# A mixture-of-experts kernel: rows loaded to places by expert, outputs in six buffers

## The chip, the cores and the metric

The kernel runs on one core of a Trainium2 chip. The time is that of one execution on the device, in microseconds (us); the kernel before took 328.78 us, the median of three runs (328.36 to 329.91). A core has five engines, each with its own queue of instructions: TensorE (PE in the profile; PEld is its weight load), VectorE (DVE), ScalarE (ACT), GpSimd (POOL) and SyncE (SP), which here only issues DMAs. Sixteen DMA engines move data between memory (HBM) and the core's SBUF. Engines wait for each other through semaphores.

## The reference

```
x = x + xattn(layernorm(x), ctx)             # x is (8, 100, 512), ctx is (8, 722, 512)
    # x1 = h @ ctx.T ; t = gelu_tanh(x1) * x1 ; result t @ ctx
x = x + ffn(layernorm(x))
    # logits = h @ router_w (512 x 16); assign = argmax(logits); w = sigmoid(top logit)
    # hh = gelu(h @ w1[assign] + b1[assign])          w1 is (16, 512, 1024)
    # out = (hh @ w2[assign] + b2[assign]) * w        w2 is (16, 1024, 512)
```

All numbers are float32. Each of the 800 tokens goes to one of 16 experts, which is known only when the kernel runs.

## The kernel before

First come eight batches of attention. For each, TensorE makes the products with the context (L316, L323), VectorE adds the residual and takes mean and variance, and the router's logits give each token its expert and its rank in the expert. GpSimd then scatters the 100 rows of the batch (values, gate, mean, inverse deviation, output row number) into `rows`, a tensor in memory with a region of 832 rows for each expert (L804). Four scatters of blank rows pad the regions (L843).

Then comes the expert stage. Work is cut into units of 32 rows of one expert. Units 0 to 3 (the head) are the first 32 rows of experts 0 to 3, read from `rows` before the last batches are done. All other units follow in the order of the experts, as many for each as it has rows. A unit j needs: its rows in SBUF; `next_tokens` (VectorE, L672), a normalization into `cur`; a transpose on TensorE (L404) and a copy to `curT` (L677); `first_layer` (L385, 32 matmuls with W1); `hidden_units` (VectorE transpose, L682), `hidden_bias` (L688), a Gelu on ScalarE (L491); `second_layer` (L396, 64 matmuls with W2); `residual_bias` (L694), which adds the gated b2 to the rows; `finish` (VectorE, L705), which writes the result to `y_out`; and a scatter to the output by GpSimd (L860). TensorE's order is first layer of j, transpose of j+1, second layer of j-1. The second layer of a unit waits until the `finish` of the unit before it has read the bank `p_y`.

Weights lie in four slots, expert e in slot e modulo 4; W1 and W2 of an expert are 2 MB each, loaded by SyncE as two halves (L232). All halves of experts 0 to 3 are loaded during the attention, as `EARLY` spreads them over the batches. In the loop at L285, W1 of an expert waits until the last unit of the slot's expert before it has passed its first layer (L291), W2 until it has passed its second (L294).

In the kernel before, each unit has its own place in `xr`, and its column in `rows` is a number that must be read from a table (`colof`). SyncE loads unit 4 (L274), GpSimd all others (L213): three for units 5 to 7, then two in each round, mixed with the output scatters. There are two output buffers. In `scatter_unit`, GpSimd waits until the scatter of two units ago has landed, frees its buffer for VectorE (`s_y_free`, L855), copies the row numbers into `out_at` (L856), waits for `finish`, and issues the scatter. In each round it then waits for the loads that it issued in this round (`s_ld`, L893) and reports two more units as landed (`s_land`, L894), for which VectorE's `next_tokens` waits (L666).

## Time and profile before

| | |
|---|---|
| median of three runs | 328.78 us |
| the profiled execution | 326.27 us |
| its span (first to last instruction) | 324.6 us |
| TensorE busy | 253.4 us (78%) |
| VectorE busy | 113.0 us (35%) |
| GpSimd busy | 89.0 us (27%) |
| ScalarE busy | 32.4 us (10%) |
| moved by DMA | 100.93 MB, mean 311 GB/s |
| weight DMAs (L232) | 64 of 1 MB |
| loads of rows of units 4 and on | 27 by GpSimd, 1 by SyncE, 66 KB each |
| output scatters (L860) | 32 |

The 64 weight DMAs are 67 MB, 48 of them for experts 4 to 15. The 32 scatters are the 32 units. The page cuts the span in 40 slices of 8.1 us, and slice 0 is the first. A row of the timeline gives the start, the time taken, the engine, the line and the tiles, and in square brackets how long the engine was idle before it and what ended that.

### The profile page before, as it was taken

What the parts mean: (1) busy time and instruction counts of PE and PEld (TensorE: products, weight loads), DVE (VectorE), ACT (ScalarE), POOL (GpSimd) and SP (SyncE); (2) the same over time, 40 slices, a digit from 0 to 9 for tenths busy, and PEclk for the clock granted to TensorE, in tenths of its full rate; (3) what the DMA queues carried; (4) which work ended last, traced back from release to release, by engine and by line L of the source; (5) the groups of instructions that cost most, each with busy time, mean ns of one, the idle gap of its engine ahead of it and who ended that gap; (6) DMA issues with size and microseconds to landing.
All of it is one profiled execution on the core that took longest, in us unless ns stands there. A gap on an engine that the chain in (4) does not pass through costs nothing. (4 is left out here: it accounts for less than half of the span.)

```text
span 324.6 us, 9969 instructions
## 1 busy us (share of the span) xinstructions
PE 253.4 (78%) x3763; PEld 179.8 (55%) x3764; DVE 113.0 (35%) x385; ACT 32.4 (10%) x76; POOL 89.0 (27%) x141
## 2 busy tenths in 40 slices
PE   1899999999999898784663747840197999899982
PEld 0868867867867456553431544520175766566762
DVE  2134444444442663242210222220043344344430
ACT  0311111112011021010000000000010111011110
POOL 1002312312341353533330234413022122221222
PEclk9999999999999959995979569895579999999998
DMA  7999899999999998753999806599759999999700
GB/s 252 377 357 361 287 371 343 385 378 342 418 381 309 420 418 327 121 182 138 291 403 361 305 25 236 176 364 375 245 209 424 424 423 426 420 421 424 289 16 14
DMA packets 21437, 100.93 MB, mean 311 GB/s; under 512 B 4942, under 2 KB 6882, under 8 KB 12200
## 3 DMA queue, kind: packets, MB, share of 16 engines
q1 hardware_dynamic: 16680, 93.81, 77.0%
q0 software_dynamic: 4592, 6.56, 6.6%
q8 instruction: 14, 0.23, 0.3%
q10 hardware_dynamic: 144, 0.27, 0.2%
q14 instruction: 7, 0.06, 0.1%
HBM read 95.89 MB, written 5.14 MB: 311 GB/s over the span
## 5 line engine op out<-in xcount | busy, mean ns | idle before, releaser
L396 PE MATMUL bank<-W,area 128*32 128x128 f32 x2048 | 76.2, 295 | 41.3 <-DVE area L705 38.5
L396 PEld LDWEIGHTS bank<-W,area 128*32 128x32 f32 x2048 | 61.9, 118 | 51.5 <-DVE area L705 40.3
L385 PE MATMUL bank<-W,area 128*32 128x256 f32 x1024 | 69.0, 409 | 14.9 <-issue 14.5
L385 PEld LDWEIGHTS bank<-W,area 128*32 128x32 f32 x1024 | 37.1, 117 | 36.8 <-issue 24.6
L860 POOL DMA_INDIRECT out<-area,out_at x32 | 32.4, 1012 | 72.1 <-DVE area L705 57.8
L316 PEld LDWEIGHTS bank<-xnT,area 128*128 128x128 f32 (+1 forms) x384 | 44.7, 194 | 4.7 <-issue 4.7
L323 PE MATMUL bank<-area,hidT 128*100 128x512 f32 (+1 forms) x96 | 46.8, 601 | 0.0
L316 PE MATMUL bank<-xnT,area 128*128 128x100 f32 (+1 forms) x384 | 45.1, 280 | 1.4 <-issue 1.4
L705 DVE SCALAR_TENSOR_TENSOR area<-bank,area 128x128 f32 (+1 forms) x28 | 9.8, 351 | 86.7 <-POOLq L855 65.8
L213 POOL DMA_DIRECT2D area<-rows x27 | 19.2, 711 | 53.5 <-issue 53.5
L491 ACT ACTIVATE area<-area 128x256 f32<-128x256 f32 x32 | 13.4, 417 | 187.6 <-PE bank L396 177.5
L682 DVE STREAM_TRANSPOSE area<-bank 128x256 f32<-128x256 f32 x32 | 14.4, 449 | 39.6 <-PE bank L385 28.4
L804 POOL DMA_INDIRECT rows<-row,pos x8 | 8.7, 1082 | 49.6 <-DVE pos L569 32.6
L323 PEld LDWEIGHTS bank<-area,hidT 128*100 128x100 f32 (+1 forms) x96 | 13.7, 167 | 10.0 <-issue 10.0
L525 DVE TENSOR_TENSOR hidT<-hidT,bank 128x300 f32<-128x300 f32 x16 | 7.4, 464 | 19.5 <-ACT hidT L463 19.5
L688 DVE TENSOR_TENSOR area<-area,b1s 128x256 f32<-128x256 f32 x32 | 13.6, 424 | 0.2 <-DVE area L682 0.2
L404 PEld LDWEIGHTS bank<-con,area 128*128 128x128 f32 x33 | 4.7, 142 | 14.7 <-issue 14.6
L672 DVE TENSOR_SCALAR area<-area 128x128 f32 (+1 forms) x28 | 9.8, 350 | 7.7 <-DMA area<-rows 3.9
L463 ACT ACTIVATE hidT<-bank 128x300 f32<-128x300 f32 x16 | 6.8, 422 | 56.4 <-PE bank L316 56.4
L792 POOL TENSOR_TENSOR rs_x<-ve_x,con 100x1 f32<-100x1 f32 x8 | 4.5, 558 | 25.9 <-DVE ve_x L511 25.9
L404 PE MATMUL bank<-con,area 128*128 128x128 f32 x33 | 11.2, 341 | 0.1
L792 POOL TENSOR_TENSOR row<-ve_t,con 100x4 f32<-100x4 f32 x8 | 8.4, 1049 | 9.2 <-DVE ve_t L511 9.0
(95 smaller groups left out, 146.0 us busy)
## 6 DMA issues: line engine op xcount, KB each, us to landing
W<-in_w SPq DMA_DIRECT2D x64, 1024.0 KB, 11.9
area<-in_ctx_main SPq DMA_DIRECT2D x8, 1280.0 KB
area<-in_ctxT_a SPq DMA_DIRECT2D x8, 768.0 KB, 8.8
area<-in_ctxT_b SPq DMA_DIRECT2D x8, 676.0 KB, 8.0
area<-rows POOLq DMA_DIRECT2D x27, 66.0 KB, 7.1
xs<-in_x SPq DMA_DIRECT2D x8, 200.0 KB
area<-in_ctx_rest SPq DMA_DIRECT2D x8, 160.0 KB
xs<-in_b SPq DMA_DIRECT2D x4, 192.0 KB
```

Source lines behind the costliest of these rows:

```text
L213: eng.dma_start(xr[:, at, :].rearrange("p o d -> p (o d)"), rows[bass.ds(col * U, U), :].rearrange("t (q d) -> q t d", q=Q)).then_inc(sign ...
L316: last = nc.tensor.matmul((p_xa, p_xb)[part][0:n, T * c:T * c + T], ctxTs[b % 2][part][:, k, P * c:P * c + n], xnT[:, k, :], start=(k == 0 ...
L323: last = nc.tensor.matmul(p_att[0:T, :], hidT[0:CW[c], c, :], cxs[b % 2][0:CW[c], c, :], start=(c == 0), stop=(c == SC - 1))
L385: last = nc.tensor.matmul(p_h[U * q:U * q + U, 0:FQ], curT[:, U * k:U * k + U], mine, start=(k == 0), stop=(k == KD - 1), tile_position=(0 ...
L396: last = nc.tensor.matmul(p_y[U * q:U * q + U, 0:DQ], hT[:, U * c:U * c + U], W2[:, slot, c, DQ * q:DQ * q + DQ], start=(c == 0), stop=(c ...
L404: nc.tensor.transpose(p_blk[:, 0:P], cur, ident).then_inc(s_blk, 1)
L491: nc.scalar.activation(hT, h_pre, ACT.Gelu).then_inc(s_act, 1)
L672: nc.vector.tensor_scalar(cur, mine[:, 0:DQ], mine[:, DQ + 1:DQ + 2], mine[:, DQ + 2:DQ + 3], ALU.subtract, ALU.mult).then_inc(s_next, 1)
L682: nc.vector.transpose(h_pre, p_h[:, 0:FQ]).then_inc(s_hT, 1)
L688: nc.vector.tensor_tensor(view, view, bias.unsqueeze(3).to_broadcast([P, 2, Q, U]), ALU.add).then_inc(s_hb, 1)
L792: nc.gpsimd.tensor_tensor(rs, ve, neg_half.to_broadcast(list(rs.shape)), ALU.pow).then_inc(s_rs, 1)
L860: nc.gpsimd.indirect_dma_start(out_q, bass.IndirectOffsetOnAxis(ap=out_at[r][:, :], axis=0), y_out[:, r, :], None, bounds_check=last_out, ...
```

## The change

- **Places.** `xr` now has a place for each expert (0 to 15), which holds the first unit of that expert that isn't a head unit, one that isn't used, and 24 places for further units (the extras). The first kind starts at a fixed row of the expert's region, so SyncE loads them without a table: `load_first`, four DMAs (one for each quarter of a row) for experts 0 to 3, four for 4 to 7, four for 8 to 15. Each waits for the pad scatters of its experts.
- **Extras.** GpSimd loads these (`load_extra`): two before scatter 1, four (`AHEAD` is 6) before scatter 2, and the rest (at least one) between scatters 3 and 4.
- **A table.** `packed` has one number for each unit, with its expert and the places of itself, of the unit before it and of the one two behind. VectorE reads it once for a unit and takes the fields out by shifts and masks. It is made by more steps in `units_of` and by a small matmul with the constant `packing` on TensorE in place of two transposes.
- **Outputs.** `y_out` and `out_at` have six buffers: one for each head unit, used once, and two for all others in turn. VectorE now copies the row numbers, in `finish`.
- **Waits.** VectorE waits for the loads at fixed points: `s_first[0]` before the tokens of unit 4, `s_extra[0]` before those of unit 5, `s_extra[1]` before unit 4, the four further extras and `s_first[1]` before unit 5, the b2 of experts 4 to 15 before unit 6, `s_first[2]` and all other extras before unit 9.
- **SyncE and GpSimd queues.** The constants (in two parts), the router, b1 (in two parts) and b2 of the head are loaded by GpSimd at the start and not by SyncE. `EARLY` has two halves less in its last entry; these two follow behind the first `load_first`.
- `b2_copy` stands behind `hidden_bias` of unit 1.

```diff
-EARLY = (0, 0, 1, 1, 1, 2, 4, 7)
+EARLY = (0, 0, 1, 1, 1, 2, 4, 5)
...
-        def load_unit(eng, j, signal):
-            at = bass.ds(j, 1) if not isinstance(j, int) else slice(j, j + 1)
+        def load_extra(eng, k, signal):
+            at, place = (slice(i, i + 1) if isinstance(k, int) else bass.ds(i, 1) for i in (k, k + E + 1))
             col = eng.value_load(colof[0:1, at], min_val=0, max_val=E * PER - 1)
-            eng.dma_start(xr[:, at, :].rearrange("p o d -> p (o d)"),
+            eng.dma_start(xr[:, place, :].rearrange("p o d -> p (o d)"),
                           rows[bass.ds(col * U, U), :].rearrange("t (q d) -> q t d", q=Q)).then_inc(signal, 16)
 
...
+            def load_first(lo, hi, skip, signal):
+                for q in range(Q):
+                    sp.dma_start(xr[U * q:U * q + U, lo:hi, :],
+                                 rows.rearrange("(e n) d -> n e d", e=E)[skip:skip + U, lo:hi, XW * q:XW * q + XW]
+                                 ).then_inc(signal, 16)
+
             sp.wait_ge(s_att, NB)
             for i in range(RB):
                 sp.wait_ge(s_row[i], 16 * len(range(i, NB, RB)))
             sp.wait_ge(s_pad[0], 16)
-            sp.dma_start(xr[:, SLOTS, :], rows[U:2 * U, :].rearrange("t (q d) -> q t d", q=Q)).then_inc(s_own[0], 16)
+            load_first(0, SLOTS, U, s_first[0])
+            load_weights(4 * SLOTS - sum(EARLY))
+            sp.wait_ge(s_pad[1], 16)
+            load_first(SLOTS, 2 * SLOTS, 0, s_first[1])
 
             sp.wait_ge(s_x2, NB)
             sp.wait_ge(s_xnps, NB)
...
+            for i in range(2, PADS):
+                sp.wait_ge(s_pad[i], 16)
+            load_first(2 * SLOTS, E, 0, s_first[2])
...
+                number = dve.value_load(packed[0:1, at], min_val=0, max_val=(1 << 22) - 1)
+
+                def field(bit):
+                    part = number // (1 << bit)
+                    return place_of(nc.s_assert_within(dve.snap(part % 64 if bit < 16 else part), 0, PLACES - 1,
+                                                       skip_runtime_bounds_check_because="places end there"))
+                return bass.ds(dve.snap(number % E), 1), field(10), field(4), field(16)
+
...
-            def finish(j, r):
+            def finish(j, mine):
+                r = dve.snap(j % 2 + SLOTS) if not isinstance(j, int) else j if j < SLOTS else j % 2 + SLOTS
                 at = slice(r, r + 1) if isinstance(r, int) else bass.ds(r, 1)
-                mine = place_of(j)
+                dve.wait_ge(s_y_free, j + 1)
                 dve.wait_ge(s_prep, j + 1)
-                dve.wait_ge(s_y_free, j + 1)
+                apart()
+                nc.vector.tensor_copy(out_at[:, at], mine[:, DQ + 3:DQ + 4].bitcast(U32)).then_inc(s_out_at, 1)
                 dve.wait_ge(s_y, j + 2)
                 apart()
...
+            dve.wait_ge(s_extra[1], 16)
+            unit(SLOTS, e4, head_of(3), place_of(0), after4)
+            dve.wait_ge(s_ahead, 16 * (AHEAD - 2))
+            dve.wait_ge(s_first[1], 16 * Q)
+            unit(SLOTS + 1, e5, before5, mine5, after5)
+            dve.wait_ge(s_b2_rest, 16 * Q)
+            with dve.Fori(SLOTS + 2, SLOTS + AHEAD - 1) as j:
+                unit(j, *unit_of(j))
+            more_loads = dve.value_load(counts[0:1, 1:2], min_val=1, max_val=EXTRA - AHEAD)
+            dve.wait_ge(s_first[2], 16 * Q)
+            dve.wait_ge(s_more, 16 * more_loads)
+            apart()
+
+            others = dve.value_load(counts[0:1, 0:1], min_val=E, max_val=E + EXTRA)
...
+            for lo, hi in ((C_ONE, C_PAD), (C_PAD, C_ALL)):
+                pool.dma_start(con[:, lo:hi], consts[:, lo:hi]).then_inc(s_conl, 16)
+            pool.dma_start(rw[:, :, :], router).then_inc(s_rw, 16)
+            for lo in range(0, E, E // 2):
+                pool.dma_start(b1s[:, lo:lo + E // 2, :], b1[:, lo:lo + E // 2, :]).then_inc(s_b1, 16)
+            pool.dma_start(b2q[:, :, :], b2[0:SLOTS].rearrange("e (q d) -> q e d", q=Q)).then_inc(s_b2, 16)
+            pool.wait_ge(s_conl, 32)
...
-            def scatter_unit(j, r, before):
-                at = slice(j, j + 1) if isinstance(j, int) else bass.ds(j, 1)
-                mine = head if isinstance(j, int) and j < SLOTS else xr
-                pool.wait_ge(s_next, j + 1)
-                if before is not None:
-                    pool.wait_ge(s_done[r], before)
-                apart()
-                if before is not None:
-                    pool.sem_inc(s_y_free, 1)
-                nc.gpsimd.tensor_copy(out_at[r][:, :], mine[:, at, DQ + 3].bitcast(U32)).then_inc(s_out_at, 1)
+            def scatter_unit(j, r, done):
                 pool.wait_ge(s_out_at, j + 1)
                 pool.wait_ge(s_yo, j + 3)
                 apart()
...
-                nc.gpsimd.indirect_dma_start(out_q, bass.IndirectOffsetOnAxis(ap=out_at[r][:, :], axis=0),
+                nc.gpsimd.indirect_dma_start(out_q, bass.IndirectOffsetOnAxis(ap=out_at[:, r:r + 1], axis=0),
                                              y_out[:, r, :], None, bounds_check=last_out, oob_is_err=False
-                                             ).then_inc(s_done[r], 16)
-
-            scatter_unit(0, 0, None)
-            pool.wait_ge(s_blank, 1)
+                                             ).then_inc(done, 16)
+
+            scatter_unit(0, 0, s_head_done)
             for i in range(RB):
                 pool.wait_ge(s_row[i], 16 * len(range(i, NB, RB)))
                 apart()
...
+            for i in range(PADS):
                 pool.wait_ge(s_pad[i], 16)
                 apart()
-
-            for j in range(2, SLOTS):
-                for k in range(2):
-                    load_unit(pool, OWN + 2 * (j - 2) + k, s_ld)
-                scatter_unit(j, j % 2, 16 * (j // 2))
-                pool.wait_ge(s_ld, 32 * (j - 1))
-                pool.sem_inc(s_land, 2)
-            n = units(pool)
-            less = pool.value_load(n_less[0:1, 0:1], min_val=SLOTS + E - NEAR - 1, max_val=MAXU - NEAR - 1)
-            loading, pairs = pool.snap(less // 4), pool.snap((less + (NEAR - 2)) // 2)
-            with pool.Fori(0, loading) as i:
+            pool.wait_ge(s_eof, 2)
+            for k in range(2):
+                load_extra(pool, k, s_extra[k])
+            scatter_unit(1, 1, s_head_done)
...
+            more_loads = pool.value_load(counts[0:1, 1:2], min_val=1, max_val=EXTRA - AHEAD)
+            with pool.Fori(AHEAD, more_loads + AHEAD) as k:
+                load_extra(pool, k, s_more)
+            pairs = pool.snap((pool.value_load(counts[0:1, 0:1], min_val=E, max_val=E + EXTRA) + 1) // 2)
+            for r in range(2):
...
+            with pool.Fori(1, pairs) as i:
                 for r in range(2):
-                    for k in range(2):
-                        load_unit(pool, 4 * i + (NEAR + 2 * r + k), s_ld)
-                    scatter_unit(2 * i + (SLOTS + r), r, 16 * i + 32)
-                    pool.wait_ge(s_ld, 64 * i + (16 * (NEAR - OWN) + 32 * r + 32))
-                    pool.sem_inc(s_land, 2)
-            with pool.Fori(4 * loading + NEAR, n) as j:
-                load_unit(pool, j, s_ld)
```

How the change moves instructions, at three places. On GpSimd, the steady loop over units before (one half of it, for one unit; L213 loads rows, L850 frees, L860 scatters):

```order
L213 DMA area<-rows 128x1x132
L850 ISA
L852 ISA
L856 ISA
L856 COPY out_at<-area 128x1
L858 REGISTER_ALU
L860 DMA out<-area,out_at 3200x128
L893 ISA
L212 ISA
L212 TENSOR_LOAD colof
```

and now, with both halves (L913 and L914 are the waits, L916 scatters):

```order
L941 ISA
L913 ISA
L914 REGISTER_ALU
L916 DMA out<-area,out_at 3200x128
L913 REGISTER_ALU
L914 REGISTER_ALU
L916 DMA out<-area,out_at 3200x128
L941 ISA
L941 COMPARE_AND_BRANCH
```

The loads, the table reads and the copy have gone from the loop. On SyncE, from the last early weights to the first weights of expert 4 before (W is the weight slots, in_b is b2):

```order
L232 DMA W<-in_w 128x2048 x11
L274 DMA area<-rows 128x1x132
L279 DMA xs<-in_b 32x12x128 x4
L285 UNCONDITIONAL_BRANCH
L285 ISA
L287 TENSOR_LOAD ends
```

and now:

```order
L249 DMA W<-in_w 128x2048 x9
L284 DMA area<-rows 32x4x132 x4
L249 DMA W<-in_w 128x2048 x2
L284 DMA area<-rows 32x4x132 x4
L300 DMA xs<-in_b 32x12x128 x4
L284 DMA area<-rows 32x8x132 x4
L309 UNCONDITIONAL_BRANCH
L309 ISA
L311 TENSOR_LOAD ends
```

Twelve row loads and two weight halves stand where one row load stood. On VectorE, the end of a unit in the steady loop before (L694 is `residual_bias`, L705 `finish`):

```order
L694 SCALAR_TENSOR_TENSOR area<-xs,area 128x128
L705 ISA x2
L705 REGISTER_ALU
L705 SCALAR_TENSOR_TENSOR area<-bank,area 128x128
L765 ISA
L765 COMPARE_AND_BRANCH
```

and now:

```order
L735 SCALAR_TENSOR_TENSOR area<-xs,area 128x128
L745 ISA x2
L745 COPY out_at<-area 128x1
L748 ISA x2
L748 SCALAR_TENSOR_TENSOR area<-bank,area 128x128
L826 ISA
L826 COMPARE_AND_BRANCH
```

The copy of the row numbers (L745) has come to VectorE.

## Rows read from the trace of the kernel before

**Rows 1.** The page, section 2: what the DMA engines moved, in 40 slices

```profile
GB/s 252 377 357 361 287 371 343 385 378 342 418 381 309 420 418 327 121 182 138 291 403 361 305 25 236 176 364 375 245 209 424 424 423 426 420 421 424 289 16 14
```

**Rows 2.** Busy time by stretch: stretch, length, engines, then PEclk, DMA share, GB/s

```profile
140.60:237.70 97.10, 52.06 (x942) 35.57 (x945) 19.89 (x60) 3.76 (x9) 27.19 (x42) 0.76 0.74 259
237.70:306.00 68.30, 62.42 (x1439) 44.33 (x1437) 29.58 (x88) 6.27 (x15) 17.44 (x29) 0.99 0.99 410
```

**Rows 3.** The waits: who, for whom, us in total, times, the longest

```profile
DVE area L705 <- POOLq L855: 65.8, 9, 20.7
...
PE bank L396 <- DVE area L705: 38.5, 10, 19.0
...
SPq L232 <- PE bank L396: 81.5, 12, 22.3
```

**Rows 4.** Timeline of GpSimd and VectorE, 177 to 189 us

```profile
177.30 0.75 POOL L213 DMA_DIRECT2D area<-rows  x1 [7.02 <-issue]
178.68 0.68 POOL L213 DMA_DIRECT2D area<-rows  x1 [0.63 <-issue]
...
179.47 0.35 DVE L705 SCALAR_TENSOR_TENSOR area<-bank,area 128x128 f32 x1 [8.33 <-POOLq L855]
...
188.24 0.74 POOL L213 DMA_DIRECT2D area<-rows  x1 [6.48 <-issue]
```

**Rows 5.** First layers from 237 us on, counted, and rows of the timeline

```profile
L385 PE MATMUL bank<-W,area x544: 376/379/634, 237.6 to 313.1; 128*32 128x256 f32 x182
...
237.65 2.89 PE L385 MATMUL bank<-W,area 128*32 128x256 f32 x32
...
298.30 1.93 PE L385 MATMUL bank<-W,area 128*32 128x256 f32 x32 [0.51 <-issue]
...
311.57 1.93 PE L385 MATMUL bank<-W,area 128*32 128x256 f32 x32 [0.47 <-issue]
...
319.19 0.35 DVE L705 SCALAR_TENSOR_TENSOR area<-bank,area 128x128 f32 x1 [2.74 <-PE bank L396]
```

**Rows 6.** Timeline at the first weight load of the loop, and its landing

```profile
140.61 0.38 SPq L232 DMA_DIRECT2D W<-in_w  x1
...
141.23 0.45 DVE L682 STREAM_TRANSPOSE area<-bank 128x256 f32<-128x256 f32 x1 [0.39 <-issue]
...
143.23 2.02 PE L385 MATMUL bank<-W,area 128*32 128x256 f32 x32 [0.38 <-issue]
...
DMA to landing us min/median/max: 9.3/9.3/9.3
```

**Rows 7.** Busy time by stretch, 126 to 140.6 us, and VectorE's timeline

```profile
126.00:134.00 8.00, 6.42 (x177) 5.10 (x181) 3.04 (x12) 0.83 (x2) 4.38 (x7) 1.00 0.92 198
134.00:140.60 6.60, 5.80 (x122) 3.38 (x110) 2.52 (x9) 0.42 (x1) 3.12 (x6) 1.00 0.26 52
...
137.78 0.45 DVE L682 STREAM_TRANSPOSE area<-bank 128x256 f32<-128x256 f32 x1 [2.47 <-issue]
```

**Rows 8.** Timeline of the full-rate stretch: `finish`, transpose, scatter and its return

```profile
262.30 0.35 DVE L705 SCALAR_TENSOR_TENSOR area<-bank,area 128x128 f32 x1 [0.88 <-PE bank L396]
...
263.49 0.98 POOL L860 DMA_INDIRECT out<-area,out_at  x1 [2.42 <-DVE area L705]
...
270.04 0.18 POOL L856 COPY out_at<-area 128x1 uint32 x1 [1.24 <-DMA out<-area,out_at]
...
276.93 0.45 DVE L682 STREAM_TRANSPOSE area<-bank 128x256 f32<-128x256 f32 x1 [0.96 <-PE bank L385]
```

**Rows 9.** Timeline: the last of four row loads, and what waited for them

```profile
224.40 0.68 POOL L213 DMA_DIRECT2D area<-rows  x1 [1.10 <-issue]
...
233.28 0.18 POOL L856 COPY out_at<-area 128x1 uint32 x1 [8.20 <-DMA area<-rows]
```

**Rows 10.** SyncE's weight loads from 237 us on, and the stretch of the stream's end

```profile
237.77 47.83 SPq L232 DMA_DIRECT2D W<-in_w  x26
...
306.00:308.00 2.00, 2.00 (x52) 1.40 (x46) 0.96 (x3) 0.42 (x1) 0.18 (x1) 1.00 0.10 33
```

More of the change, by code:

```diff
@@ L422, in _ @@
             first_layer(2, 2, 16)
-            pe.wait_ge(s_tab, 10)
+            pe.wait_ge(s_tab, 16)
             pe.wait_ge(s_pos, NB)
-            for i in range(2):
-                last = nc.tensor.transpose(p_rk[0:1, 64 * i:64 * i + MAXU], unit_f[:, i:i + 1], ident[0:MAXU, 0:MAXU])
-            last.then_inc(s_eofps, 1)
+            nc.tensor.matmul(p_rk[0:1, 0:MAXU], unit_f[:, 0:1], ident[0:MAXU, 0:MAXU], start=True, stop=False)
+            nc.tensor.matmul(p_rk[0:1, 0:MAXU], unit_f[:, 1:2], packing, start=False, stop=True)
+            nc.tensor.matmul(p_rk[0:1, 64:64 + EXTRA], unit_f[:, 2:3], picked[:, :], start=True, stop=True
+                             ).then_inc(s_eofps, 1)
             transpose_tokens(3)
@@ L723, in _ @@
             pads()
-            b2_copy()
             units_of()
@@ L758, in unit @@
                 hidden_bias(j, e)
-                next_tokens(j + 2)
-                residual_bias(j, e)
-                finish(j - 1, (j + 1) % 2 if isinstance(j, int) else dve.snap((j + 1) % 2))
-            for j in range(SLOTS, OWN - 2):
-                unit(j)
-            with dve.Fori(OWN - 2, last) as j:
-                unit(j)
-            e = expert_of(last)
+                next_tokens(j + 2, following)
+                residual_bias(e, mine)
+                finish(j - 1, before)
+            dve.wait_ge(s_extra[1], 16)
[11 more added lines that the diff above has]
+            others = dve.value_load(counts[0:1, 0:1], min_val=E, max_val=E + EXTRA)
+            last = others + (SLOTS - 2)
+            with dve.Fori(SLOTS + AHEAD - 1, last) as j:
+                unit(j, *unit_of(j))
+            e, before, mine, _ = unit_of(last)
             hidden_units(last)
@@ L895, in _ @@
-            with pool.Fori(4 * loading + NEAR, n) as j:
-                load_unit(pool, j, s_ld)
-            pool.wait_ge(s_ld, 16 * less + 16 * (NEAR + 1 - OWN))
-            pool.sem_inc(s_land, 4)
-            with pool.Fori(loading, pairs) as i:
-                for r in range(2):
-                    scatter_unit(2 * i + (SLOTS + r), r, 16 * i + 32)
+            pool.wait_ge(s_eof, 2)
+            for k in range(2):
+                load_extra(pool, k, s_extra[k])
+            scatter_unit(1, 1, s_head_done)
```

190 lines of the change are left out of this document (105 added, 85 removed).

## The prediction

> **What bounds the kernel now.** I read the slices of the page first, then the waits, the busy times by stretch, and the timeline around the longest waits.
>
> The GB/s row [rows 1] splits the run in three: some 120 us of attention, most slices above 340; a stretch up to slice 29 (243 us) in which it keeps falling, once to 25; and 60 us at 424 GB/s. The middle stretch, 140.6 to 237.7 us, has the TensorE busy for 52 of 97 us and the DMA at 0.74 of its time; the next one has 0.99 and 410 GB/s [rows 2]. So the expert stage is not bound by weights until 237 us; something else holds it there.
>
> The waits name it [rows 3]: VectorE's `finish` (L705) waited 65.8 us for GpSimd's queue at L855, the increment that frees an output buffer; TensorE's second layer waited 38.5 us for that `finish`; and SyncE's weight loads waited 81.5 us for that second layer. The timeline shows one round, which is one unit [rows 4]: GpSimd issues two loads at 177.30 and 178.68 us, and only behind them frees the buffer, so L705 runs at 179.47 after 8.33 us idle; then comes the scatter, and then GpSimd waits until both loads have landed, so the next round starts at 188.24, 10.9 us later. Behind 237.7 us no loads are left and the pace is another one: 544 L385 matmuls are 17 first layers of 32, the first at 237.65 and the last at 311.57 us [rows 5]. That is 73.9 / 16 = 4.62 us for a unit, and there the same two output buffers are in use.
>
> **What the change removes.** GpSimd no longer mixes loads with scatters, no longer copies the row numbers (VectorE does), and the wait for `s_ld` before releasing rows is gone. Of the 28 loads of rows, 16 come by SyncE in 12 DMAs, 12 by GpSimd, six of these before unit 4 and six in one piece before scatter 4. By the routing of these inputs (from the reference) the experts have 2,1,1,4,1,1,1,2,1,3,1,2,2,2,3,1 units behind the four head units; expert 0's last is unit 5, expert 3's unit 11, and expert 14's first unit 28. If the hold-up is gone, late are (a) TensorE at 4.62 us a unit, (b) the weights of experts 4 to 15, 48 DMAs of 1.049 MB, which start when unit 5 has left its first layer (140.61 us before, [rows 6]).
>
> **The front, up to the first weight load.** Two of the sixteen early weight DMAs move behind the attention, about 5 us of DMA (2.1 MB at 424 GB/s), and their consumer, the second layer of unit 3, ran at 135.6 us. The row loads of SyncE are 1.06 MB in pieces of 528 B. The nearest rows are the b2 pieces and row loads between 126 and 134 us: 198 GB/s at a share of 0.92; from 134 to 140.6 us the share was 0.26, 4.9 us of it free [rows 7]. Bounds for 1.06 MB: 2.5 us at 424 GB/s and 5.3 us at 198; less 1.9 us for the loads that it replaces there. I take 5, most of which the free 4.9 us hide. Unit 4's token wait is unlikely to grow, since the last row scatter has 5 us less of weights ahead. VectorE waited 2.47 us before the transpose of unit 4 at 137.78 [rows 7] on the b2 pieces; that wait moves behind unit 5, and two table reads (about 1 us each by the 0.96 us before L682 in the steady loop, [rows 8]) stand in its place. First layer of unit 5: unchanged, ends at 140.4. But before unit 5's transpose (141.23 us, [rows 6]) VectorE now waits for four loads that GpSimd issues behind scatter 1, at about 131.5 to 136.2 us (1.16 us apart). Four loads with weights in flight took until 233.28 us after the last issue at 224.40 [rows 9], 8.9 us; with nothing in flight about 7. So they land at 143 to 145: a wait of 2 to 4 us, I take 3. The first-layer start of unit 6 goes from 143.23 to 146.2, and its second layer for unit 5 ends 4.3 us later at 150.5.
>
> The constants, router and biases go by six GpSimd DMAs at about 7 to 13 us instead of SyncE's queue. Their reader is free until 16.7 us; I cost it at nothing, bounds 1 us gained (0.45 MB less ahead of the second batch) and 2 us lost.
>
> **The unit loop.** The added copy on VectorE is at most 0.25 us and 4 register operations; it stands before the wait for the second layer, which was 0.88 us long [rows 8]. Price 0; if that cover were gone, 26 x 0.25 = 6.5 us. The stretch with six loads in one piece: GpSimd issues them from 143 to 151 us (1.38 us each in its loop, from 177.30 to 178.68 [rows 4]), scatters 4 and 5 at 151 and 152.5 us. Unit 6 needs scatter 4 landed. In the full-rate stretch a scatter issued at 263.49 us released GpSimd at 270.04 [rows 8], 6.5 us; with loads ahead 8.9 at most. So `finish(6)` runs at about 160 us against 153 by pace: one wait of 7 us. Then first layer of unit 9 at 162.4, of unit 31 at 162.4 + 22 x 4.62 = 264. From that start to the end of the span 324.6 - 311.57 = 13.0 us [rows 5]. TensorE's bound: 277 us of span.
>
> **The weight stream.** The W2 of expert 4 may go when the second layer of unit 5 is done, 150.5, issue at 150.8. The two DMAs of a tensor on an idle queue took 9.3 us to land [rows 6], the second issued 0.5 later: W2 of expert 4 is there at 160.6. Afterwards full rate: from 237.77 us 26 DMAs were issued and the stream ended at about 306 us [rows 10], 28.0 MB in all at 410 GB/s including the ramp, 424 without it [rows 1]; outputs take 3 in 100 of that, so 1.049 / 0.412 = 2.54 us for one. Up to the W1 of expert 14 are 19 more tensors, 38 x 2.54 = 96.5; the six loads cost 0.6 us each (the DMA dropped from 424 to about 310 GB/s for 8 us around four of them, slices 27 and 28 [rows 1]), 3.6. It lands at 160.6 + 96.5 + 3.6 = 260.7 us. No slot is late: expert 3's slot is free at about 173.5 us, its turn comes near 180. Unit 28 can begin its first layer some 0.5 us before (the wait is by halves), and from 298.30, unit 28 before, to the end were 26.3 us [rows 5]. Span: 260.7 - 0.5 + 26.3 = 286.5 us.
>
> So the weights, not TensorE (277), set the end. The profiled execution of before took 326.27 us, 1.67 over its span, and the median of the three is 328.78, 2.5 more. 286.5 + 1.7 = 288.2 us profiled, 290.7 beside the median. Since the front has more small gains than I booked (a shorter wait for unit 4's rows, 1.7 us), I say **289 us**; its own range 283 to 296.
>
> The Trainium skill, DMA: Bandwidth & Descriptors, section Specifications, gives an HBM limit of about 358 GB/s for a core. The trace disagrees: 420 to 426 GB/s for 55 us [rows 1]. By the page a DMA of weights would last 2.93 us, the 40 up to expert 14's W1 cost 16 us more, and the time would be 305.
>
> The same page, Anatomy of one DMA, fits a GpSimd DMA as 2.0 us plus its bytes at 436 GB/s, an estimate of 2.2 us for a scatter of 66 KB. The trace shows 6.5 us under load [rows 8]. By the page the output ring could never bind and the 7 us wait at unit 6 would be none, which leaves the sum as it is, since the weights are later.
>
> **The rivals.**
> - *TensorE is the bound.* The front loses nothing (3 us), the loads cost no DMA time (3.6 us), the stream starts by 145 us. Then 277 to 279 of span, **282 us**. For it: much of the first tensor's 9.3 us may be waiting behind the small pieces. Against: expert 14's three units stand right behind their weights.
> - *The front collides.* SyncE's queue reaches the first weight only behind 12 row loads and 4 b2 loads, and the small pieces run at 120 GB/s instead of 198 (128 to 136 us before had 154). 8.8 + 5 us of work against 4.9 free, and the four loads land at 149: unit 5 waits 8 us, the stream starts 8 late. **298 us**.
> - *The output ring binds, on the slower side.* Each pair of units now waits for the scatter of two units ago: 0.35 finish + 1.2 to the issue + landing + 0.4. With 6.5 us that is 8.5, under 2 x 4.62 = 9.24. With more it sets the pace: finish 29 would come at 164 + 12 pairs, and finish 31 and the end (5.4 us behind it, 319.19 to 324.6, [rows 5]) right after. A landing of 9.3 us, as the weights had, gives 11.3 per pair and 309 us of time; 11 us gives 13.0 and 329, the time of before; from there on the kernel is slower, at 12.5 us 14.5 and **347 us**. For it: the 8.9 us at the loads, with weights in flight. Against: between 240 and 306 us the stream had no gap either, and scatters were back in 6.5 us.
> - *The stream runs at 358 GB/s*: **305 us**, against the rate seen here.
>
> **Chances.** Forecast 0.58, TensorE 0.18, collision 0.16, 358 GB/s 0.01, ring 0.07, of which 0.04 slower and 0.02 within 0.5%. The range, 280 to 303, takes the first three. A measurement tells 0.5% (1.6 us). Faster 0.94, within 0.5% 0.02, slower 0.04.
>
> **What would show it.** Right: L705 hardly waits for GpSimd but once, around 155 us, for 5 to 9 us; DMA above 415 GB/s from about 155 to 268 us; first layers 4.6 us apart on the mean; the last 26 us as before; one wait of 2 to 4 us ahead of unit 5's transpose. Wrong: waits of L705 for GpSimd in many units (the ring), DMA holes past 160 us (slots free late), a first weight load after 145 us (the front), or first layers that never wait for a DMA (TensorE).

## The result, and the profile after

The changed kernel takes **296.05 us** (median of 4 runs, 293.97 to 298.72), the kernel before 329.35 (328.36 to 335.05) beside it: a ratio of 0.898, 95% interval 0.890 to 0.906. The forecast was 289 us with a range of 280 to 303. The profiled execution is the longest of the four, 298.72 us with a span of 296.2 (the others 292.3 to 295.3); it counts as a slow run, as does the 335.05 us of the kernel before, and the ratio leaves both out. At the median the time missed the forecast by 7 us. The trace is of the long execution, and its span is 9.7 us over the forecast's span of 286.5 us; the terms below are for these 9.7 us, and up to 3.9 of them are its own excess over its fellows.

The page's GB/s row, 40 slices of 7.4 us, is the one to set against [rows 1]:

```profile
GB/s 232 378 382 361 295 332 391 378 355 366 364 420 387 329 395 412 227 342 168 86 340 330 416 417 281 287 370 422 424 424 420 423 422 423 418 422 424 343 17 7
```

The full rate no longer begins at slice 30 (243 us) but at slice 27 (200 us), and nearly at slice 22 (163 us); between them two slices stand at 281 and 287. Busy time by stretch (columns as in [rows 2]) shows the same with the engines:

```profile
140.60:160.00 19.40, 14.94 (x299) 10.65 (x303) 6.16 (x22) 1.25 (x3) 8.26 (x10) 0.85 0.78 242
160.00:180.00 20.00, 14.91 (x323) 10.28 (x317) 6.73 (x22) 1.25 (x3) 2.05 (x3) 0.90 1.01 401
180.00:200.00 20.00, 17.15 (x407) 12.08 (x403) 10.10 (x32) 1.67 (x4) 4.74 (x5) 1.00 0.80 302
200.00:280.00 80.00, 70.44 (x1597) 48.94 (x1593) 36.82 (x115) 7.08 (x17) 15.52 (x16) 0.96 1.01 422
```

The weight stream (the DMAs of weights, one behind the other) is the bound from 200 us on: 422 GB/s for 80 us. The waits that held the kernel before [rows 3] have these successors (L745 and L748 are the two operations of `finish`, L409 the first layer, L420 the second, L249 the weight load):

```profile
PE bank L409 <- issue: 19.6, 16, 4.3
...
PE bank L409 <- DMA W<-in_w: 3.0, 3, 1.6
...
DVE out_at L745 <- POOLq L945: 5.1, 2, 4.0
...
DVE area L714 <- DMA area<-rows: 4.3, 1, 4.3
```

```profile
SPq L249 <- PE bank L420: 46.3, 11, 8.2
...
SPq L249 <- PE bank L409: 21.7, 4, 10.1
```

`finish` waits 5.1 us for GpSimd instead of 65.8, and TensorE's second layer waits for `finish` only 1.4 us in all, against 38.5. The first layers now wait for weights, three times and 3.0 us in all: 0.87 us in unit 26, 0.57 and 1.57 us in unit 28. So the weights set the end, but with TensorE close behind. SyncE's weight loads still wait for TensorE, 10.1 us at most; the question is whether the DMA engines run dry meanwhile. The front, by the timeline:

```profile
139.36 0.34 DVE L714 TENSOR_SCALAR area<-area 128x128 f32 x1 [4.34 <-DMA area<-rows]
...
143.76 1.90 PE L409 MATMUL bank<-W,area 128*32 128x256 f32 x32
...
145.88 1.30 SPq L249 DMA_DIRECT2D W<-in_w  x2
```

VectorE waited 4.34 us for the first of GpSimd's loads (issued at 129.1), which landed 9.7 us after its issue, so the first layer of unit 5 and the first weight load behind it are some 5 us later than before (145.88 against 140.61, [rows 6]). Then comes the stretch in which TensorE falls behind:

```profile
152.37 12.42 SPq L249 DMA_DIRECT2D W<-in_w  x8
...
156.34 2.92 PE L409 MATMUL bank<-W,area 128*32 128x256 f32 x32 [4.04 <-issue]
156.92 1.04 POOL L916 DMA_INDIRECT out<-area,out_at  x1 [0.92 <-issue]
...
165.85 0.15 DVE L745 COPY out_at<-area  x1 [3.98 <-POOLq L945]
...
168.11 2.36 PE L409 MATMUL bank<-W,area 128*32 128x256 f32 x20 [4.31 <-issue]
...
172.85 1.91 PE L409 MATMUL bank<-W,area 128*32 128x256 f32 x32
```

Unit 7's first layer starts 4.04 us late at 156.34, and unit 8's stops after some of its matmuls and goes on at 168.11, 4.31 us later. Both waits are "issue": no semaphore that the profile shows ended them. `finish(6)` waits 3.98 us for a scatter that was issued at 156.92, behind the six row loads, and came back 8.9 us later. Unit 9 starts at 172.85. Now units 11 and 12 (the last of expert 3, and the one behind it), the weight loads in the same time, and the DMA engines:

```profile
181.81 1.93 PE L409 MATMUL bank<-W,area 128*32 128x256 f32 x32
...
187.56 1.93 PE L409 MATMUL bank<-W,area 128*32 128x256 f32 x32 [1.59 <-issue]
...
189.69 1.95 PE L420 MATMUL bank<-W,area 128*32 128x128 f32 x64
```

```profile
183.95 0.94 SPq L249 DMA_DIRECT2D W<-in_w  x2
...
191.70 0.81 SPq L249 DMA_DIRECT2D W<-in_w  x2
```

```profile
182.00:187.00 5.00, 3.97 (x97) 2.72 (x89) 2.76 (x9) 0.53 (x2) 0.97 (x1) 1.00 0.52 156
187.00:190.00 3.00, 2.44 (x45) 1.43 (x49) 0.37 (x1) 0.00 (x0) 0.97 (x1) 1.00 1.01 426
190.00:195.00 5.00, 4.52 (x122) 3.39 (x117) 2.11 (x8) 0.42 (x1) 0.97 (x1) 1.00 0.66 215
```

The W1 slot of expert 3 is free when unit 11's first layer is through, 183.7, and its next load leaves at 183.95; the W2 slot when unit 11's second layer is through (the 64 L420 from 189.69 on), and its load leaves at 191.70. Each time the queue had drained: the rate of the stretch is 156 and 215 GB/s, and 3.1 and 2.5 us of stream are lost, 5.6 in the two holes together. The end, to set against [rows 5]:

```profile
263.42 1.07 PE L409 MATMUL bank<-W,area 128*32 128x256 f32 x16 [0.57 <-DMA W<-in_w]
...
266.06 1.69 PE L409 MATMUL bank<-W,area 128*32 128x256 f32 x16 [1.57 <-DMA W<-in_w]
...
279.20 1.93 PE L409 MATMUL bank<-W,area 128*32 128x256 f32 x32 [0.45 <-issue]
...
287.06 0.35 DVE L748 SCALAR_TENSOR_TENSOR area<-bank,area 128x128 f32 x1 [1.58 <-PE bank L420]
288.25 0.97 POOL L916 DMA_INDIRECT out<-area,out_at  x1 [2.26 <-DVEq L845]
```

Unit 28 waits for its W1 by halves, as forecast, but it starts at 263.42 us, where the sum had 260.2, and its second half waits until 266.06. From unit 31's start the end is 17.0 us away; before it was 13.0. GpSimd's last instruction, a DRAIN, takes 5.46 us from 290.54 on; before it took 1.70 us.

### The profile page after: what moved, and what is told of

Read it like the earlier page. It is cut to its first block, busy times and chain, and to the rows that moved or that the text cites. A ratio compares the mean times of both kernels' runs of the same rounds, so it can differ in the third digit from the quotient of the medians.

```text
span 296.2 us, 9809 instructions
## 1 busy us (share of the span) xinstructions
PE 245.5 (83%) x3767; PEld 174.1 (59%) x3768; DVE 120.7 (41%) x425; ACT 32.4 (11%) x76; POOL 74.0 (25%) x99
## 4 chain that ended last, share of the span: by engine, by line
PE 70%; DMA 13%; issue 9%; DVE 2%; SPq 2%; POOL 1%; DVEq 0%; POOLq 0%
PE bank L409 17%; PE bank L420 17%; PE bank L340 15%; PE bank L347 14%; DMA W<-in_w 9%; DMA area<-rows 3%; PE bank L428 2%; PE bank L355 1%; SPq L249 1%; PE bank L325 1%; DMA xs<-in_x 1%; PE bank L331 1%; PE bank L363 0%; DVE area L724 0%; PE bank L362 0%
## 5 line engine op out<-in xcount | busy, mean ns | idle before, releaser
L409 PE MATMUL bank<-W,area 128*32 128x256 f32 x1024 | 68.6, 408 | 22.8 <-issue 19.6
L420 PE MATMUL bank<-W,area 128*32 128x128 f32 x2048 | 70.4, 282 | 6.8 <-issue 5.3
L420 PEld LDWEIGHTS bank<-W,area 128*32 128x32 f32 x2048 | 58.2, 113 | 14.9 <-issue 9.6
L409 PEld LDWEIGHTS bank<-W,area 128*32 128x32 f32 x1024 | 36.1, 115 | 44.0 <-issue 27.0
L916 POOL DMA_INDIRECT out<-area,out_at x32 | 31.3, 978 | 117.4 <-DVE area L748 113.6
L748 DVE SCALAR_TENSOR_TENSOR area<-bank,area 128x128 f32 (+1 forms) x28 | 9.8, 351 | 10.2 <-issue 5.5
L230 POOL DMA_DIRECT2D area<-rows x12 | 8.4, 703 | 10.7 <-issue 10.7
L325 PE MATMUL bank<-con,xs 100*128 100x100 f32 x32 | 4.5, 265 | 7.4 <-DVE xs L544 7.4
```

The lines of the kernel that those rows point to most:

```text
L409: last = nc.tensor.matmul(p_h[U * q:U * q + U, 0:FQ], curT[:, U * k:U * k + U], mine, start=(k == 0), stop=(k == KD - 1), tile_position=(0 ...
L420: last = nc.tensor.matmul(p_y[U * q:U * q + U, 0:DQ], hT[:, U * c:U * c + U], W2[:, slot, c, DQ * q:DQ * q + DQ], start=(c == 0), stop=(c ...
L748: nc.vector.scalar_tensor_tensor(out=y_out[:, at, :].rearrange("p o d -> p (o d)"), in0=p_y[:, 0:DQ], scalar=mine[:, DQ:DQ + 1], in1=mine[ ...
L916: nc.gpsimd.indirect_dma_start(out_q, bass.IndirectOffsetOnAxis(ap=out_at[:, r:r + 1], axis=0), y_out[:, r, :], None, bounds_check=last_ou ...
```

## The experiments

Two theories on the stream. **H**: TensorE is some 10 us late at unit 9, so expert 3's slots (the expert with most units) come free late, the DMA engines run dry at 182 and 190 us, and since the stream is the bound behind them, each us lost there is a us at the end. **R**: the end is set by rate and row loads alone, and the holes are made up for. On the last 4 us: **D**, GpSimd's drain is longer because it writes nothing itself in the loop any more. Each kernel below ran in four executions; the kernel before ran beside them, at 328.26 us with kernels 1, 3, 4 and 5, 327.67 with 2, 6, 7 and 8, and 321.81 with 9 to 12. The changed kernel itself ran in none of these rounds. Between groups, then, neither ratios nor differences of 1 or 2% in time say much, and the traces have to carry the comparison.

The table gives, for the profiled execution of the changed kernel and of the experiments made from it: when the weight stream's first load was issued, how many us it lost between 160 and 200 us (40 x (1 - GB/s / 422), from the rate in that window), their sum, the first us in which the DMA was below 150 GB/s at the end, the span, and the drain with the number of GpSimd's DMAs.

| kernel | median us (range) | first load | lost | sum | stream's end | span | drain us (DMAs) |
|---|---|---|---|---|---|---|---|
| changed kernel | 296.05 (293.97–298.72) | 145.9 | 6.7 | 152.6 | 280 | 296.2 | 5.46 (66) |
| two buffers | 296.09 (294.70–296.82) | 143.9 | 6.8 | 150.7 | 279 | 292.6 | 5.46 (66) |
| last six loads by SyncE | 294.45 (294.08–294.65) | 153.9 | 0.1 | 154.0 | 278 | 292.6 | 4.97 (60) |
| late b2 | 295.11 (293.88–297.05) | 144.4 | 6.3 | 150.7 | 281 | 295.3 | 5.46 (66) |
| loads in pairs | 296.78 (295.56–299.96) | 143.1 | 7.0 | 150.1 | 280 | 293.9 | 5.54 (67) |
| early list as before | 296.66 (293.19–298.62) | 140.9 | 7.1 | 148.0 | 277 | 291.5 | 5.46 (66) |
| GpSimd write | 295.38 (295.09–295.88) | 144.1 | 6.5 | 150.6 | 279 | 293.2 | 5.46 (66) |
| delay in unit 9 | 304.06 (303.91–304.95) | 142.9 | 15.3 | 158.2 | 287 | 302.5 | 5.46 (66) |
| delay in unit 14 | 293.45 (292.78–294.86) | 145.6 | 5.3 | 150.9 | 279 | 293.1 | 5.46 (66) |
| constants by SyncE, early list | 292.52 (289.58–295.40) | 141.4 | 4.8 | 146.2 | 275 | 287.9 | 4.96 (60) |
| constants and last six by SyncE | 295.35 (294.91–297.04) | 156.2 | 0.0 | 156.2 | 280 | 293.3 | 4.48 (54) |

**1. The kernel before with the scatter ahead of the loads.** The loads' landing is waited for two rounds later.

```
+ pool.wait_ge(s_ld[r], 32 * i + 32); pool.sem_inc(s_land, 2)   # now ahead of the scatter
  scatter_unit(2 * i + (SLOTS + r), r, 16 * i + 32)
+ for k in range(2): load_unit(pool, 4 * i + (NEAR + 2 * r + k), s_ld[r])   # was ahead of it
```

> The kernel before with one thing altered: in GpSimd's rounds the output scatter goes first and the two loads of rows behind it, and a pair of loads is waited for two rounds later, not in its own round. Places by unit, the load of unit 4 by SyncE alone and two output buffers stay. Theory L (the gain came from taking the loads' landing out of the buffer's way): most of it is here too, 298 to 306 us, since only the loads' issue (1.4 us each) and a scatter landing behind loads (about 9 us a pair of units) are left in nine rounds. Rival P (fixed places, SyncE and six buffers carry it): 315 us or more.

Measured: 314.48 us (310.51 to 315.76), ratio 0.954 (0.945 to 0.963). What is left of the wait sits in one place, as the waits of this kernel say:

```profile
DVE area L705 <- POOLq L855: 31.9, 4, 23.8
```

That is 31.9 us against 65.8 [rows 3], with 23.8 at once, at unit 13, where GpSimd waits for the last four loads before it frees a buffer. So the order of loads and scatters is part of the gain, but not the half of it (13.8 of 33 us). The time is at the bound of rival P's 315 us and far from L's 298 to 306.

**2. The same with that last wait one pair of scatters later.**

```
- pool.wait_ge(s_ld[2], ...); pool.sem_inc(s_land, 4)           # here before
  with pool.Fori(loading, loading + 1) as i: scatter_unit(...) x2
+ pool.wait_ge(s_ld[2], ...); pool.sem_inc(s_land, 4)
```

> The kernel before with scatters ahead of loads as in the first experiment, and the wait for the last four loads moved behind one more pair of scatters. In the first experiment one wait of finish for that moment was 23.8 us of the 31.9 in all. Theory L (taking the landing out of the buffer's way is the gain): 294 to 299 us, the changed kernel's time with none of its places, table and buffers. Rival P: the stream would fill the gap anyway, 308 us or more.

Measured: 307.17 us (305.40 to 313.22), ratio 0.935 (0.926 to 0.944); its waits:

```profile
DVE area L705 <- POOLq L855: 25.9, 5, 16.0
```

L's 294 to 299 us did not come; P's 308 missed by 0.8. 16 us at once remain, again behind the landing of loads in GpSimd's order. Still, about 20 of the 33 us come with this much, with none of the places, the table or the six buffers, so taking the loads out of the way of the output buffers is the larger part of the gain. The other 11 to 13 us were not separated further.

**3. The changed kernel with two output buffers instead of six.**

```
- r = j % 2 + SLOTS        # finish: four buffers of their own for units 0 to 3
+ r = j % 2
- pool.sem_inc(s_y_free, SLOTS + 2)
+ pool.sem_inc(s_y_free, 2)
```

> The changed kernel with two output buffers for all units in place of six. Theory L: the four head buffers hide only landings while little else is late, so 296 to 299 us against 296. Rival B (the buffers carry a good part): GpSimd waits for scatters 0 and 1 before it frees units 2 and 3, each some 8 us, and the first weight load starts late: 304 us or more.

Measured: 296.09 us, ratio 0.901 (0.895 to 0.908). The waits for a buffer grow to

```profile
DVE out_at L745 <- POOLq L953: 8.9, 3, 7.2
```

and the time doesn't, as theory L had it. The six buffers are worth nothing here that these runs can tell (the interval is 0.7% to either side), and the rival of the output ring falls with them.

**4. The last six row loads by SyncE, ahead of the weight loop.**

```
+ sp.wait_ge(s_eof, 2)                 # SyncE, ahead of its weight loop
+ with sp.Fori(AHEAD, more_loads + AHEAD) as k: load_extra(sp, k, s_more)
- with pool.Fori(AHEAD, more_loads + AHEAD) as k: load_extra(pool, k, s_more)
```

> The changed kernel with the six last extras loaded by SyncE ahead of its weight loop and not by GpSimd between scatters 3 and 4. Theory H (TensorE, late by ten microseconds at unit 9, frees expert 3's slot late, and the two holes that this opens in the weight stream at 182 and 190 us move the end one for one): the 4 us wait of finish for a buffer at unit 6 goes, the holes shrink by about 4 us, 290 to 293 us. Rival R (the end is set by the rate of the stream and what the row loads cost it, the holes are filled up anyway): 295 to 297 us.

Measured: 294.45 us, ratio 0.897 (0.891 to 0.903). Timeline of SyncE, and the window 160 to 200 us:

```profile
141.15 11.45 SPq L230 DMA_DIRECT2D area<-rows  x6
153.92 2.16 SPq L249 DMA_DIRECT2D W<-in_w  x4
```

```profile
160.00:200.00 40.00, 33.51 (x797) 24.98 (x798) 17.96 (x56) 3.33 (x8) 7.71 (x8) 1.00 1.01 421
```

The stream starts 8 us later and loses nothing between 160 and 200 us, and the kernel ends no later. So the changed kernel's early start is given back in the holes. Two things close them here: the slots' turn comes later, and TensorE is through unit 11's first layer at 177.22 us instead of 183.7, since its waits in units 7 and 8 are 2.89 and 2.80 us instead of 4.04 and 4.31 (L413 is the first layer here):

```profile
152.67 2.71 PE L413 MATMUL bank<-W,area 128*32 128x256 f32 x32 [2.89 <-issue]
...
162.42 1.50 PE L413 MATMUL bank<-W,area 128*32 128x256 f32 x23 [2.80 <-issue]
```

The time lies between H's 290 to 293 us and R's 295 to 297.

**5. b2 of the later experts by ScalarE, later.** The four b2 loads leave SyncE's queue and are issued by ScalarE behind its unit 4.

```
- sp.dma_start(b2s[U * q:U * q + U, SLOTS:, :], ...)    # SyncE
+ act.dma_start(b2s[U * q:U * q + U, SLOTS:, :], ...)   # ScalarE, behind gelu_unit(4)
```

> The changed kernel with the b2 of experts 4 to 15 (four DMAs in pieces of 512 bytes) issued by ScalarE behind unit 4's Gelu and waited for before unit 9, not by SyncE at 127 us. Theory H: the extra load that unit 5 waits for lands 3 to 4 us earlier, all of units 5 to 11 come as much earlier, the stream starts earlier and the holes stay: 292 to 294 us. Rival R: the b2 pieces now take their DMA time from the weight stream, nothing gained: 296 to 299 us.

Measured: 295.11 us, ratio 0.898 (0.891 to 0.905): VectorE still waits 4.3 us for its row load, and the holes stay (6.3 us). The b2 pieces do not make the front late, so H's 292 to 294 us, which rested on that, did not come, nor did R's 296 to 299.

**6. The six loads in pairs behind scatters 3, 4 and 5** instead of in one piece, so that `finish(6)` gets its buffer sooner.

```
  for r in range(2):
      scatter_unit(SLOTS + r, SLOTS + r, s_done[r])
+     for k in range(AHEAD + 2 + 2 * r, AHEAD + 4 + 2 * r): load_extra(pool, k, s_mid)
```

> The changed kernel with the six last extras in three pairs, behind scatters 3, 4 and 5, and one more load behind them; VectorE waits for the six before unit 9. SyncE's queue stays as in the changed kernel, so the first weight load keeps its place at about 146 us. Theory H: no wait of finish for a buffer at unit 6, units 9 to 11 some 4 us earlier, expert 3's slot free earlier, the holes in the stream at 182 and 190 us about half as long: 291 to 294 us. Rival F (the 4 us are under the stall of unit 8's first layer, in which TensorE waits for no semaphore at all, and come back nowhere): 295 to 297 us.

Measured: 296.78 us, ratio 0.908 (0.900 to 0.916). The longest wait of `finish` for a buffer falls from 4.0 to 1.1 us and unit 9 still starts at 172.6 (172.85 in the changed kernel): that wait lay beside TensorE's own stall in unit 8 and cost nothing. This is rival F's number and reason; H's 291 to 294 us had taken unit 9 to be 4 us earlier.

**7. The early list of weight loads as before** (seven instead of five in its last entry).

```
- EARLY = (0, 0, 1, 1, 1, 2, 4, 5)
+ EARLY = (0, 0, 1, 1, 1, 2, 4, 7)
```

> The changed kernel with EARLY as before: all sixteen early weight DMAs are issued by the end of the attention. Theory Q (the extra load of unit 5 lands 10 us after its issue since 2 MB of weights and the small pieces go at the same time): the rows' scatters land later by up to 3 us, but the load for unit 5 is as late as without, 295 to 298 us. Rival: the two halves are what makes it late, then unit 5 starts 4 us earlier and the time is 291 to 293 us.

Measured: 296.66 us with a wide range (293.19 to 298.62), ratio 0.906 (0.899 to 0.913): no difference that these runs can tell. The median is where theory Q had it; the profiled execution, the fastest of the four at 293.19, is nearer to the rival: the stream starts 5.0 us earlier (140.9) and ends 3 us earlier.

**8. A write by GpSimd ahead of each scatter of the loop.**

```
+ nc.gpsimd.memset(touched[:, :], 0.0).then_inc(s_touch, 1)
+ pool.wait_ge(s_touch, 2 * i + (r - 1))
```

> The changed kernel with one small write of GpSimd to SBUF ahead of each output scatter of its loop. The last instruction of GpSimd, a drain, takes 5.46 us in the changed kernel, 1.70 us before, where GpSimd copies the row numbers in its loop; in three kernels it was 82.7 to 82.8 ns for each DMA that GpSimd had issued (66, 66 and 60 DMAs: 5458, 5458 and 4968 ns). Theory D (an ordinary GpSimd instruction between DMAs settles this as it goes): drain at 1.7 to 2.3 us, 292 to 293 us. Rival (the drain hangs on something else): 5.46 us again, 296 us.

Measured: 295.38 us, ratio 0.901 (0.895 to 0.906), drain 5.46 us as without it. Theory D falls.

**9 and 10. A delay on VectorE, in unit 9 or in unit 14.** Ten writes of 128x600 to an idle tile between the hidden copy and the token copy; all else is the same.

```
  hidden_units(j)
+ for k in range(10):
+     nc.vector.memset(idle[:, :], 0.0).then_inc(s_idle, 1)
+     dve.wait_ge(s_idle, k + 1)
  tokens(j + 1)
```

> The kernel after the change with ten writes of 128x600 zeros to a tile of their own on VectorE between the hidden copy and the token copy of unit 9, each waited for; some 6 us of work by VectorE's rate on plain copies, so TensorE's first layer of unit 10 starts about 4 to 6 us later than its 176.9. Theory H (TensorE's lateness at the units of experts 3 and 4 keeps a weight slot busy and opens holes in the weight stream, and each us of hole moves the end by one): the holes grow by the delay, the last first layers and the end move by 4 to 6 us, span about 297 to 300 beside 292 to 296. Theory R (the end is set by the stream and row loads with room to spare, the holes are filled up later): the end moves by at most 1 us.

> The same delay in unit 14 instead, ahead of the first layer of unit 15. Theory H: the slots that these units hold are also on the way of the weight stream, but after expert 5's units TensorE has had time to draw level; the weight stream waits for fewer of its slots, so the end moves less than with the delay at unit 9, by 0 to 2 us. A rival (any lateness of TensorE, wherever it lies, moves the end by its own size, as TensorE is the bound): 4 to 6 us in both places. Theory R: at most 1 us in both.

Measured: 304.06 us (303.91 to 304.95) and 293.45 us (292.78 to 294.86), on the same chip in the same rounds. Both delays reach TensorE. In unit 9, by the timeline, and the window 160 to 200 us:

```profile
182.05 0.56 DVE L830 MEMSET idle<- 128x600 f32 x1 [0.19 <-DVE idle L830]
...
182.99 3.64 PE L410 MATMUL bank<-W,area 128*32 128x256 f32 x32 [7.23 <-DVE area L720]
...
189.21 1.90 PE L410 MATMUL bank<-W,area 128*32 128x256 f32 x32
```

```profile
160.00:200.00 40.00, 25.95 (x509) 16.67 (x505) 17.38 (x47) 2.50 (x6) 4.85 (x5) 0.83 0.66 261
```

And in unit 14:

```profile
205.63 3.64 PE L410 MATMUL bank<-W,area 128*32 128x256 f32 x32 [6.21 <-DVE area L720]
...
211.34 1.91 PE L410 MATMUL bank<-W,area 128*32 128x256 f32 x32
```

```profile
160.00:200.00 40.00, 33.03 (x748) 23.12 (x744) 17.90 (x53) 2.91 (x7) 6.79 (x7) 0.94 0.92 366
...
200.00:270.00 70.00, 59.09 (x1390) 41.53 (x1390) 37.31 (x112) 6.25 (x15) 13.59 (x14) 0.95 1.01 422
```

TensorE is held for 7.23 us in the one and 6.21 in the other, and in both the next first layer takes 3.64 us, twice its usual 1.9. Yet beside the second the first costs 10.0 us more of stream (15.3 lost against 5.3) and 9.4 us more of span. The second leaves the stream at 422 GB/s. R said at most 1 us in both, the rival "TensorE is the bound" 4 to 6 in both; only H has the two apart. H's size was too small by some 4 us: the delay was longer than I had reckoned (ten writes and their waits take 7.3 us), and the matmuls behind the pause ran slower.

What the delay in unit 14 cost by itself is less sure, as no undelayed kernel ran beside it and the kernel before was 2% faster in these rounds. Its trace shows that it used up what TensorE had to spare: not one first layer waits for weights any more (3.0 us in the changed kernel), unit 28 starts at 264.49 us, and the stream ends at 279 as elsewhere. By this a longer delay there would move the end; none was tried.

**11 and 12. Fewer DMAs on GpSimd.** Constants, router, b1 and the first b2 go by SyncE; in 11 with the early list as before, in 12 with the last six row loads by SyncE as in 4.

```
- pool.dma_start(con[...], ...) x2; pool.dma_start(rw, ...); pool.dma_start(b1s[...], ...) x2; pool.dma_start(b2q, ...)
+ sp.dma_start(...)                                      # the same six, among SyncE's first loads
```

> The kernel after the change with the constants, the router, b1 and the first b2 loaded by SyncE among the early loads (6 fewer loads on GpSimd, as before the change) and the early weight list as before. GpSimd issues 60 DMAs, so its drain at the end should take 60 x 82.7 ns = 4.96 us beside 5.46; first layer of unit 5 near 139 to 141 as in the run with the early list alone. If these add up: 294 to 295 us, spans about 291. If the loads by SyncE push the early rows back: 296 to 298.

> The kernel after the change with both the constants and the last six row loads by SyncE (54 DMAs on GpSimd: drain 54 x 82.7 ns = 4.47 us). The weight stream starts near 153 and should then run without a hole to about 278, as in the run with the row loads alone by SyncE (294.45 us). Theory H: the same time less the 0.5 to 1.0 us of drain, 293.5 us. If the drain does not count by the number of DMAs: 294.5, with 5.46 us of drain.

Measured: 292.52 us (289.58 to 295.40) and 295.35 us (294.91 to 297.04). The drains are as expected, 4.96 and 4.48 us. Kernel 11 is 2 us better than expected, kernel 12 1.9 worse than H had it; its stream lost nothing but started at 156.2 instead of 153, and its first layers (L420 here) wait 15.3 us for weights. Its TensorE waits in units 7 and 8 are the shortest of all:

```profile
151.77 1.93 PE L420 MATMUL bank<-W,area 128*32 128x256 f32 x32 [2.10 <-issue]
...
157.88 1.50 PE L420 MATMUL bank<-W,area 128*32 128x256 f32 x23 [0.80 <-issue]
```

Kernel 11 has the earliest end of all, yet its range covers that of the delayed kernel 10 beside it, so I don't call it faster than the changed kernel, which did not run in these rounds.

## Why the forecast came out as it did

The mechanism was right in the main: the weights, not TensorE or the output ring, set the end; the stream runs at 420 GB/s and above once it runs freely; unit 28 waits for its W1 by halves; `finish` has one long wait for GpSimd (3.98 us at 165.85, where 5 to 9 us near 155 were forecast, and 1.1 us more at the end). But two of the signs that the forecast had named for being wrong appeared too: DMA holes past 160 us, and a first weight load after 145 us (145.88; 142.9 to 145.6 in kernels 3, 6, 8, 9 and 10, which have the same front). The time, 296.05 us, is at the edge of the forecast's own range of 283 to 296. And the margin was thin: the sum had TensorE's path 9.5 us shorter than the weights' (277 against 286.5), while the measured first layers waited for weights 3.0 us in all. The 9.7 us are three terms of the sum.

- **"No slot is late: expert 3's slot is free about 173.5 us, its turn comes near 180"** failed, and is the step that was wrong in kind. The turn came at about 182, the slot at 183.7. The stream lost 6.7 us between 160 and 200 us, 5.6 of them in the two holes, which the sum had at nothing; the sum had booked 3.6 for the row loads, of which 1.1 is left over in that window. Net: **3 us or so**. The slot was late because the sum took unit 9 at 162.4 us, with one wait of `finish` ahead of it; it came at 172.85. The wait was there (3.98 us), but beside it stood TensorE's two waits of 4.04 and 4.31 us without a semaphore, 8.4 together, and a front that was 2.0 us later than the sum had it (unit 6 at 148.23 against 146.2). Such waits were in the profile of before too, as waits of L385 for "issue" (14.5 us in 15 waits, the longest 2.8), and I had read them as nothing. The six loads were mis-sized as well: 1.62 us apart and not 1.38, so scatter 4 left at 156.92 and not at 151.
- **The front** was booked with 3 us of wait, hidden for the first weight load at 140.6. It was issued at 145.9; the W2 of expert 4 followed at 152.37 instead of 150.8: **1.6 us**. The late one was the first of GpSimd's loads, needed by unit 5, not the four behind it, which I had priced. With the same front the first load scatters from 142.9 to 145.9 us over the profiled executions, so part of this term may be no more than the one execution.
- **The end** from unit 31 on, taken from before as 13.0 us, was 17.0, of which 3.8 are GpSimd's drain: **4.0 us**. No row of before could show this.

Their sum, 8.7, leaves about 1 us. Experiments 9 and 10 show the first term's mechanism, and 4 and 12 its other side: where the start is late and TensorE early, the holes are gone. In the table the stream's end is the sum column plus 124 (the two kernels without holes) to 130 us; that the others lie 3 to 6 above fits the gap between their first two loads and the next (152.37 in the changed kernel), which the window from 160 us doesn't cover; no run separates it.

Of the rivals, the collision in the front had the right sign and about the right time (298), and the measured 296.05 is nearer to it than to the forecast. That is mostly luck: of the 8 us it named, the first weight load was 5.3 us late and the W2 of expert 4 only 1.6, and the rest of the miss lies in the slots and at the end. TensorE as the bound is against the changed kernel's waits for weights, and a pure form of it against kernels 9 and 10; it came within 3 us of being so. The ring is excluded by kernel 3, 358 GB/s by the 422 here. On the rate the Trainium skill, DMA: Bandwidth & Descriptors, section Specifications, differs from the trace again: it puts the limit of a core at about 358 GB/s, and the measurement decides.

Open: what TensorE's waits in units 7 and 8 are. They stand in every kernel made from the changed one, in experiments 1 and 2, and in the kernel before in unit 8 alone (2.79 us); all "issue" waits ahead of first layers come to 11.6 to 20.6 us in sum. They are shorter where the weight stream starts later. In kernel 12, with its first load at 156.2, they are 2.10 and 0.80 us; in kernel 4, at 153.9, 2.89 and 2.80; in all others of the family, at 140.9 to 145.9, 3.9 to 5.3 and 3.3 to 4.3. Instruction packets of the DMA (16 KB) run at 152.6, 159.1, 165.6, 172.2 and 178.2 us in the changed kernel, some 6.5 us apart, and none from there to the end of the span; in kernel 12 the two at 151.7 and 155.6, ahead of its stream, are 3.9 us apart. So instructions that arrive late beside the weights would fit both, but no run isolates it. Open too: why the drain was 1.70 us in the kernel before.

## What to carry to other kernels

When a wait goes away and a stream of weights becomes the bound, lay the time at which each slot comes free beside the time at which its turn comes, and with a margin: here the forecast had 6.5 us of it, and lateness of 10 us in an earlier unit used it up. A us of TensorE's lateness where the DMA queue is about to run dry is a us at the end; the same lateness five units later left the stream whole and took only what TensorE had to spare. Starting the stream earlier is worth little if it then waits for the same slot. A path that was 9.5 us from being the bound in the sum was 3 us from it in the trace: take the second bound's terms as seriously as the first's. And the end of the program is a term of its own: here GpSimd's drain took 5.46 us of it.

## What the runs showed of the hardware

- In the changed kernel and the ten made from it, GpSimd's drain at the end goes with the number of DMAs it issued: 54, 60, 66 and 67 of them took 4.48, 4.96 to 4.97, 5.46 and 5.54 us, 82.7 to 82.9 ns each. Only the direct DMAs varied (10 to 23); the 44 scatters are in all. It is no general price: with 75 DMAs the drain was 1.70 us in the kernel before and 2.27 in experiments 1 and 2.
- A row load whose address comes from a table costs 1.62 us of GpSimd's time in its loop (four timeline rows from 150.46 to 155.32) and 2.16 us of SyncE's (kernel 4, six loads from 141.15 to 151.95).
- Behind six row loads and beside weights (293 to 418 GB/s from 156 to 166 us), a scatter of 66 KB came back 8.9 us after its issue; the nearest row of before was 6.5 [rows 8].
- Behind TensorE's pauses of 7.23 us (kernel 9) and 6.21 us (kernel 10) the granted clock was at its lower level, 1.2 GHz (0.50 of full from 184 to 188 and from 204 to 208 us), and a first layer took 3.64 us instead of 1.90.
